# Cross-attention on one core: the softmax numerators change partitions by SBUF-to-SBUF transfers instead of a trip through HBM

## What is computed

```python
memory_proj = einsum('bme,de->bmd', memory, W_mem)
scores = einsum('bnd,bmd->bnm', hidden_states, memory_proj) / sqrt(D)
attn = softmax(scores, axis=-1)
memory_context = einsum('bnm,bmd->bnd', attn, memory_proj)
gate_input = concatenate([hidden_states, memory_context], axis=-1)
gate = sigmoid(einsum('bnf,df->bnd', gate_input, W_gate) + b_gate)
fused = hidden_states + gate * memory_context
return rmsnorm(fused, norm_w)
```

## Time and profile before

| what | value |
|---|---|
| median of 3 runs | 1637.91 us (1637.56 to 1638.33) |
| the profiled execution | 1638.24 us |
| its span, first to last instruction | 1636.5 us |
| TensorE, matmul busy | 1581.6 us, 97% |
| TensorE, weight loads (beside matmuls) | 1303.7 us, 80% |
| VectorE | 1034.8 us, 63% |
| ScalarE | 456.6 us, 28% |
| DMA traffic | 259.33 MB, 158 GB/s |
| stores of numerators | 128 of 256 KB, 2.7 us to landing (median) |
| reads of numerators | 128 of 256 KB, 4.3 us to landing (median) |

### The profile page before, as it was taken

How to read it: one execution, slowest core, us unless ns; L and a number is a source line. 1 busy time by engine, 2 the same in 40 slices (tenths; PEclk the granted TensorE clock), 3 DMA queues, 4 the chain that set the end, 5 groups by cost and what they waited for, 6 DMA issues and landing times.

```text
span 1636.5 us, 21429 instructions
## 1 busy us (share of the span) xinstructions
PE 1581.6 (97%) x6912; PEld 1303.7 (80%) x6912; DVE 1034.8 (63%) x1423; ACT 456.6 (28%) x763; POOL 17.9 (1%) x37
## 2 busy tenths in 40 slices
PE   6898899999999979999999999999999999999998
PEld 5687688888888768888888888888888888888886
DVE  5463567777777754467436754575445767776776
ACT  4222233222222332235322532244223211111111
POOL 0000000000000000000000000000000000000000
PEclk9899999999999989999999999999999999999999
DMA  9879763333332675757594658566555544545452
GB/s 175 184 189 239 163 160 109 110 103 112 116 114 98 154 184 160 179 154 198 146 202 133 174 145 199 146 174 179 159 172 158 162 170 171 176 160 170 167 179 97
DMA packets 188888, 259.33 MB, mean 158 GB/s; under 512 B 15040, under 2 KB 113344, under 8 KB 188608
## 3 DMA queue, kind: packets, MB, share of 16 engines
q1 hardware_dynamic: 188864, 259.06, 57.3%
HBM read 168.82 MB, written 88.08 MB: 157 GB/s over the span
## 4 chain that ended last, share of the span: by engine, by line
issue 99%; POOLq 0%; POOL 0%; DVE 0%; DVEq 0%
POOL rstd L556 0%; POOLq L554 0%; DVE region_f L1219 0%; POOLq L556 0%; DVEq L50 0%; POOL minus_half L552 0%; POOLq L1418 0%
## 5 line engine op out<-in xcount | busy, mean ns | idle before, releaser
L1245 PE MATMUL bank<-region_t,region_l 128*128 128x512 f32 x3072 | 704.9, 390 | 5.5 <-DVE region_l L247 3.3
L1245 PEld LDWEIGHTS bank<-region_t,region_l 128*128 128x128 f32 x3072 | 576.9, 188 | 129.1 <-issue 9.5
L1245 PE MATMUL bank<-region_n,region_l 128*128 128x512 f32 x1536 | 354.8, 390 | 6.0 <-DVE region_l L247 6.0
L1245 PEld LDWEIGHTS bank<-region_n,region_l 128*128 128x128 f32 x1536 | 289.2, 188 | 66.5 <-DVE region_l L247 6.4
L1245 PE MATMUL bank<-region_t,region_n 128*128 128x512 f32 x960 | 226.3, 399 | 33.0 <-DVE region_t L247 25.8
L1245 PEld LDWEIGHTS bank<-region_t,region_n 128*128 128x128 f32 x960 | 185.4, 194 | 73.5 <-DVE region_t L247 14.3
L693 ACT CAST region_l<-bank 128x512 fp32r<-128x512 f32 x128 | 75.1, 586 | 337.0 <-DVE bank L1032 336.8
L212 DVE STREAM_TRANSPOSE region_f<-region_f 128x512 f32<-128x512 f32 (+3 forms) x85 | 121.0, 1426 | 69.9 <-DMA region_f<-in_x 42.9
L1032 DVE STREAM_TRANSPOSE bank<-region_f 128x512 f32<-128x512 f32 x128 | 88.8, 716 | 120.3 <-DMA region_f<-prob_scratch 118.1
L1286 PE MATMUL bank<-region_t,region_l 128*128 128x512 f32 x576 | 135.7, 389 | 0.0
L247 DVE TENSOR_TENSOR region_t<-region_f,region_t 128x1024 fp32r<-128x1024 f32 (+2 forms) x70 | 102.2, 1491 | 41.8 <-ACT region_t L568 34.4
(11 more groups left out here) (57 smaller groups left out, 830.7 us busy)
## 6 DMA issues: line engine op xcount, KB each, us to landing
region_f<-in_x SPq DMA_DIRECT2D x64, 512.0 KB, 4.5
region_f<-in_ctx SPq DMA_DIRECT2D x128, 256.0 KB, 5.5
prob_scratch<-prob SPq DMA_DIRECT2D x128, 256.0 KB, 2.7
region_f<-prob_scratch SPq DMA_DIRECT2D x128, 256.0 KB, 4.3
region_f<-in_x SPq DMA_DIRECT2D x128, 128.0 KB, 2.7
region_f<-zx_scratch SPq DMA_DIRECT2D x32, 512.0 KB, 3.6
out<-region_f SPq DMA_DIRECT2D x31, 512.0 KB, 2.8
q_scratch<-prob SPq DMA_DIRECT2D x8, 1024.0 KB, 9.9
```

The source lines that it names most:

```text
L1245: mm = nc.tensor.matmul(dst, lhs(a), rhs(b), start=first and n == 0, stop=last and n == len(PASSES) - 1)
```

## The change

`exchange` no longer goes through HBM. Block j is moved by four DMAs from SBUF to SBUF: source are the 32 partitions of row group b and the 512 columns of block j, target are the 32 partitions of group j and the columns 512 b to 512 b + 511 of `b_px`. They are issued as soon as the exponentials of block j are done. The HBM array and the semaphores `p_stored` and `px_loaded` go; `px_moved[j]` counts landings, and the three places that waited for the old ones wait for it.

```diff
             def exchange(unit, first=False):
-
-                def there(j):
+                for j in range(MB):
                     sp.wait_ge(exp_done, unit * MB + j + 1)
-                    cols = slice(BANK * j, BANK * (j + 1))
-                    sp.dma_start(prob_dram[unit, :, cols], prob[:, cols]).then_inc(p_stored[j], 16)
-
-                def back(j):
-                    sp.wait_ge(p_stored[j], (unit + 1) * 16)
                     if j == 0 and not first:
                         sp.wait_ge(pt_t, unit * MB)
-                    sp.dma_start(b_px[SQ * j:SQ * (j + 1)].rearrange("i (b m) -> i b m", b=TPB),
-                                 prob_dram[unit, :, BANK * j:BANK * (j + 1)].rearrange("(b i) m -> i b m", i=SQ)
-                                 ).then_inc(px_loaded, 16)
-
-                there(0)
-                there(1)
-                for j in range(2, MB):
-                    there(j)
-                    back(j - 2)
-                back(MB - 2)
-                back(MB - 1)
+                    for b in range(TPB):
+                        sp.dma_start(b_px[SQ * j:SQ * (j + 1), BANK * b:BANK * (b + 1)],
+                                     prob[SQ * b:SQ * (b + 1), BANK * j:BANK * (j + 1)]).then_inc(px_moved[j], 16)
...
             for j in range(MB):
-                sp.wait_ge(p_stored[j], 16 * NUNIT)
+                sp.wait_ge(px_moved[j], 16 * TPB * NUNIT)
             sp.dma_start(c_nw, norm_w.rearrange("(a d) -> a d", a=1).to_broadcast([P, D])).then_inc(nw_loaded, 16)
...
                     for j in range(MB):
-                        act.wait_ge(p_stored[j], unit * 16)
+                        act.wait_ge(px_moved[j], unit * (16 * TPB))
...
-                dve.wait_ge(px_loaded, (i + 1) * (16 * NQ))
+                for j in range(MB):
+                    dve.wait_ge(px_moved[j], (i + 1) * (16 * TPB))
```

More of the change, by code:

```diff
@@ L44, in build @@
     am_dram = nc.dram_tensor("am_scratch", [NUNIT, P, TPB * CHC], F32).ap()
-    prob_dram = nc.dram_tensor("prob_scratch", [NUNIT, P, M], F32).ap()
     zx_dram = nc.dram_tensor("zx_scratch", [ROWS, D], F32).ap()
@@ L174, in build @@
         exp_done, sum_done, inv_done = sem("exp_done"), sem("sum_done"), sem("inv_done")
-        p_stored = [sem(f"p_stored{j}") for j in range(MB)]
-        px_loaded = sem("px_loaded")
+        px_moved = [sem(f"px_moved{j}") for j in range(MB)]
         pt_t, pt_hi, pt_ready = sem("pt_t"), sem("pt_hi"), sem("pt_ready")
```

## The result

The changed kernel takes **1660.42 us** (median of four executions, 1658.17 to 1663.69), beside 1638.12 for the kernel before. The medians lie 22.3 us apart; the ratio of the executions is 1.0141, with an interval of 1.0127 to 1.0155. The change makes the kernel slower. The profiled execution took 1663.69 us, with a span of 1661.9, so it lies 25.45 above the profiled execution of before (1638.24).

The account below looks back on a forecast made before the run. TensorE, busy 97% of the span, was taken as the bound, so only its waits could be won. First unit -2.86 and units 8, 16, 24 -1.2 gave -4.1 on 1638.24, or 1633.9 us at the median; range 1632.0 to 1642.0.

Parts of the forecast that it names:

- Their price decides all: Eight more SyncE issues a unit, taken 0.48 us apart, without the address computation of loops; SyncE busy 8.0 us, 7.57 before.
- Removed round trip, calm loop: Steps without extra waits: one queue round trip fewer, all landed in 9.9 us (10.84 before); some 0.9 shorter, buying nothing itself.
- Units 3, 11 and 19: Where twelve memory loads follow the step: the attention output, not the exchange, still decides when they start; 0.
- Units 8, 16 and 24: Last two memory blocks load behind the exchange: issued 0.5 us later, but landing faster without 256 KB reads ahead; -1.2 us.
- The first unit: Unit 0: first transpose starts 2.86 us earlier, waiting for VectorE's own splits instead of the transfer back; -2.86 us.
- The first rival: Dearer issues make SyncE the bound at units 3, 11, 19; at 0.56 us an issue +4.2, 1642.1 us; chance 0.25.
- The second rival: Exchange transfers serialize at some 0.93 us each, loop 25.7 us; +118 over 30 units, 1756 us; chance 0.04.

Follow-up runs that it names:

- The first two runs: Changed kernel moving half of each exchange's bytes: sixteen transfers of 32 KB a unit, 1658.55 us; then eight transfers of 64 KB, 1635.84 us.
- The quarter stores: Kernel before the change, each 128-partition store to HBM cut into four of 32 partitions, twenty issues a unit: 1746.08 us, beside 1638.84.

## Why the prediction was wrong

**The step that failed** is "Their price decides all", and in it "An SBUF address needs no such step, so I take 0.48". The issues are 0.63 us apart and hold SyncE for 10.2 us, where 8.0 was taken. The first half of the sentence holds, as only 0.04 us lies between two issues. What it had too small is the issue itself, 0.59 us, where the stores and loads of the rows have 0.34 and 0.43. The text had both ends of the range in hand: 0.44 for loads out of HBM, and 0.93 for the one SBUF-to-SBUF row. It took the price from the rows of another kind and set the one row of this kind aside for its bytes, 32 times as many, and the queue ahead of it. The first two runs show that bytes do not set the price. The quarter stores show that the form alone does not, since the same 32 partitions cost 0.315 to HBM. The kind sets it, SBUF at both ends, and with it the form (0.47 for 128 partitions, 0.59 for 32). Why such an issue is dearer no run shows. The stated upper end of 0.93 was even wide enough, but the range of the time stopped at 0.56.

**Removed round trip, calm loop** "some 0.9 us shorter": it became 0.65 longer. The landing was better than thought (2.0 for 2.4, and 0.22 more to the transpose), but fifteen steps of 0.63 are 9.45, where the working had 7.2: 11.66 us from the first transfer to the transpose, where 9.9 was forecast.

**Units 3, 11 and 19**, "0": +21.3 us, the largest error. The sentence "the shorter loop brings them up to 1.8 us forward: the attention output (832.12) still decides" turned over in both of its parts, as the loop got longer and the hold too. Unit 11's stores were 3.34 us late. Besides, the sum had no term for the query load, which lands 0.4 to 1.0 us later than before in these three units, nor for TensorE's clock.

**Units 8, 16 and 24**, "-1.2": +8.0. The loads go out 2.8 us later, not 0.5. The gain counted against this came, and it was larger: ScalarE gets the eighth load 11.2 us after the first one's issue in unit 24, where it was 13.4 (2.1 less, 1.2 taken). So the loads are ready only 0.6 us later against the exchange. How the rest of the 8.0 comes about was not taken apart; the waits go when one of the two blocks is loaded ahead of the exchange.

**The first unit**, "-2.86": the mechanism is as told, as the transpose waits for VectorE's splits and not for a transfer. The size is -1.8, from the start of the exponentials to the transpose (17.09 before, 15.27 after). VectorE's splits ended later against these exponentials than in the trace of before, by 1.1 us, since the last of the memory loads landed later. The sum had taken the rest of the work as fixed. The gain itself is no accident of one trace: the transpose starts 16.7 to 17.4 us after the exponentials in the three traces with the old exchange, and 15.1 to 15.3 in the six with twelve or sixteen small transfers and no copies of GpSimd. The runs with eight and with twelve transfers, in which SyncE is held no longer than before, come out at -0.22% and -0.18%, 3.6 and 2.9 us. This is near the gain side of the sum, -4.1, but it does not confirm its terms: the profiled execution with twelve transfers lies 0.4 us under that of before, and its attention output of unit 31 0.2 us behind, as the wait at unit 3 takes the first unit's gain.

**The first rival** was the one that came: the same mechanism, the same places, and its signs (stores that start when the exchange ends, waits of over 1.5 us). Its size was somewhat short: its own working with 0.63 gives some +17, an estimate, and the loss is 22. It counted the lateness of SyncE once for each of three places. It left out that the lateness grows on its way (3.34 us late at the stores, but 4.2 more of waiting in unit 11, with slower issues and the late landing of the query), and that TensorE comes back at the lower clock, 7.6 us over the three. The second rival, transfers that serialize, is refuted: they overlap, and 64 KB land 2.0 us after issues 0.63 apart. The rule of the Trainium skill ("DMA: Bandwidth & Descriptors", rules for kernel authors), to coalesce small transfers, as one pays mostly overhead, points the right way here, and the runs agree: halving the bytes changed the price of an issue by nothing, and halving the count at equal bytes won 22.7 us. They do not agree with the time worked out from that page, 15.2 us for an exchange and a loss of over 100 us: the overhead was SyncE's 0.63 us an issue, and the transpose starts 11.66 us after the first transfer.

## What to carry to other kernels

When one DMA becomes several, count the issues on the queue and list what is queued behind them, before looking at bytes. Take the price of an issue from a row with the same source and target memory and the same number of partitions, and if the only such row is the dear one, let it set the upper end of the time too. A burst of loads behind a step turns a little lateness of the queue into a long wait; spread over the steps, the same loads cost nothing, and the change that lost 22 us became the fastest complete kernel of this document, ahead of the old exchange with the same loads by an amount that is not sharp. Price a long wait of TensorE with the slower set behind it. Before an idle engine is given work, look at what runs beside it on VectorE.

## What was not expected of the hardware

- An issue on SyncE takes 0.59 us for 32 partitions from SBUF to SBUF (64, 32 and, as 0.58, 16 KB), 0.47 for 128 partitions, and 0.315 to 0.333 from SBUF to HBM in either form.
- The same 64 KB in 32 partitions lands 1.6 us after its issue in HBM and 2.0 in SBUF. The Trainium skill ("DMA: Bandwidth & Descriptors", Anatomy of one DMA) puts most of the fixed time on the target's receipt, heaviest for HBM. It says so of DMAs that GpSimd issues; these are SyncE's. With 32 partitions the traces do not agree, and with 128 they do (2.7 us to HBM in the kernel before, 2.3 to SBUF in the run with four transfers), but the queues were not loaded alike.
- TensorE's sets of 48, which take 11.04 us, were slower behind all 20 waits of 3.24 to 7.85 us in the attention stages of thirteen traces (the quarter stores left out): 12.5 to 14.1 us. Where the windows were read, the granted clock was 0.50 at first. Behind 19 waits of 1.93 to 2.96 us four sets were slower (12.7) and fifteen not (11.1 to 11.2), with 2.06 and 2.07 us on both sides; behind the 21 waits of 1.33 to 1.71 none was.
- A lo half of 128 x 512 takes VectorE 0.69 us alone and mostly 1.32 us while GpSimd copies 32 x 512 blocks with an addition.
